# First stage of a decoder layer: weights and x in halves, other loads later, zero products and one SiLU ahead

## The reference

```
v = silu(dwconv_causal(x @ v_w.T, convv_w))      # 4 taps per channel, 256 channels
short = dwconv_causal(v, fir_s)                   # 3 taps
# long_ and wide: 31 and 64 taps of the same v; then delta rule on q, k, v, gate, mixing
x = layernorm(x + attn(x)); x = layernorm(x + xattn(x, ctx)); x = layernorm(x + ffn(x))
```

## Time and profile before

| what | value |
|---|---|
| median of three runs | 664.91 us (664.7 to 665.05) |
| profiled execution: span from first to last instruction | 663.7 us |
| the profiled execution's own time | not given apart; the median is 1.2 us above its span |
| first matmul / first ACT work / first DVE work | 7.64 / 11.45 / 13.58 us |
| PE starts the second stage | 61.47 us |

### The profile page before, as it was taken

How to read it: one execution, slowest core, us unless ns; L and a number is a source line. 1 busy time by engine, 2 the same in 40 slices (tenths; PEclk the granted TensorE clock), 3 DMA queues, 4 the chain that set the end, 5 groups by cost and what they waited for, 6 DMA issues and landing times.

```text
span 663.7 us, 16965 instructions
## 1 busy us (share of the span) xinstructions
PE 570.7 (86%) x7446; PEld 409.4 (62%) x7446; DVE 464.9 (70%) x898; ACT 281.7 (42%) x510; POOL 118.1 (18%) x102
## 2 busy tenths in 40 slices
PE   4886889898998999887998867799999799879983
PEld 1454567676767667765544445688888665446542
DVE  1986857867786787854859999364266875676674
ACT  1766545433452344332365542333322545444541
POOL 1001520250061016000011223353000000000000
PEclk9898979999999999987999888799999899989998
DMA  6600710330051014120421117100000000000001
GB/s 182 222 3 2 232 55 4 122 105 4 8 178 44 4 34 129 35 99 34 172 84 32 33 32 243 32 1 0 1 1 1 1 0 1 1 32 1 33 21 44
DMA packets 26536, 37.50 MB, mean 57 GB/s; under 512 B 4641, under 2 KB 13602, under 8 KB 26463
## 3 DMA queue, kind: packets, MB, share of 16 engines
q1 hardware_dynamic: 26463, 36.42, 17.1%
HBM read 34.31 MB, written 2.10 MB: 55 GB/s over the span
## 4 chain that ended last, share of the span: by engine, by line
PE 20%; DVE 17%; ACT 6%; issue 6%; POOL 1%; POOLq 0%; DVEq 0%
PE bank L1805 6%; PE bank L1787 3%; PE bank L1862 2%; DVE arena L2502 2%; DVE arena L2509 2%; PE bank L1876 2%; ACT arena L2192 2%; ACT arena L2194 1%; DVE arena L2279 1%; PE bank L1908 1%; DVE arena L149 1%; ACT short L2098 1%; DVE arena L2318 1%; PE bank L1808 1%; PE bank L690 1%
## 5 line engine op out<-in xcount | busy, mean ns | idle before, releaser
L298 DVE SCALAR_TENSOR_TENSOR arena<-bank,conv_w,arena 128x511 f32<-128x511 f32 (+2 forms) x72 | 53.1, 746 | 17.3 <-ACT arena L457 14.0
L1523 POOL COPY arena<-v_win 128x256 f32<-128x256 f32 x32 | 20.2, 660 | 171.7 <-PE bank L775 171.7
L2055 ACT COPY arena<-bank 128x512 f32<-128x512 f32 x40 | 23.3, 584 | 56.0 <-PE bank L1805 37.1
L1805 PE MATMUL bank<-v_win,arena 128*128 128x256 f32 x192 | 46.0, 389 | 0.0
L1920 PE MATMUL bank<-v_win,arena 128*128 128x256 bf16 x288 | 36.1, 277 | 8.3 <-DVE arena L2522 7.3
L1190 ACT COPY arena<-bank 128x512 f32<-128x512 f32 x40 | 21.7, 589 | 48.2 <-PE bank L901 48.2
L1805 PEld LDWEIGHTS bank<-v_win,arena 128*128 128x128 f32 x192 | 37.3, 196 | 5.6 <-issue 0.4
L1787 PE MATMUL bank<-v_win,arena 128*128 128x256 f32 x128 | 33.5, 425 | 7.7 <-DVE arena L2348 4.4
L775 PE MATMUL bank<-arena 128*32 128x128 f32 x512 | 35.7, 409 | 4.9 <-ACT arena L1140 3.1
L1908 PE MATMUL bank<-arena,v_win 128*128 128x512 bf16 x144 | 35.9, 386 | 3.8 <-DVE arena L2502 1.7
L1920 PEld LDWEIGHTS bank<-v_win,arena 128*128 128x128 bf16 x288 | 28.1, 99 | 17.1 <-DVE arena L2522 8.2
(11 more groups left out here) (284 smaller groups left out, 1345.0 us busy)
## 6 DMA issues: line engine op xcount, KB each, us to landing
arena<-in_toep_w SPq DMA_DIRECT2D x32, 256.0 KB, 3.0
arena<-in_toep_l SPq DMA_DIRECT2D x32, 256.0 KB, 3.9
arena<-in_xT SPq DMA_DIRECT2D x12, 512.0 KB, 4.7
arena<-in_x SPq DMA_DIRECT2D x4, 512.0 KB, 4.0
arena<-in_ctx SPq DMA_DIRECT2D x4, 512.0 KB, 4.2
out<-arena SPq DMA_DIRECT2D x4, 512.0 KB, 2.9
qkv_w<-in_qkv_wT SPq DMA_DIRECT2D x1, 768.0 KB, 5.4
v_win<-in_w_gateT SPq DMA_DIRECT2D x1, 768.0 KB, 4.7
```

What stands on the lines that cost most here:

```text
L298: return nc.vector.scalar_tensor_tensor(out=acc[:, j:L], in0=src[:, 0:L - j], scalar=conv_w[:, m, CONV_K - 1 - j:CONV_K - j], in1=acc[:, j:L],
L1805: i = mm(oo, src[:, k, f * P:(f + 1) * P], w[:, k, :], start=(k == 0), stop=(k == KT - 1 and f > 0))
L2055: nc.scalar.copy(dst(i), bank[RING_FIRST + n % RING].rearrange("p (t c) -> p t c", c=dst(i).shape[-1]))\
```

## The change

The changed kernel issues the first loads in another order and in smaller pieces, each with its own semaphore:

- The value columns of the weights and x of batch 0 are fetched in halves by channel group k (128 KB and 256 KB), and PE's first projection waits for each half just before the matmul that reads it.
- `conv_w` stands between the halves; `short_w` and the identity come after x of batch 1. ACT and DVE wait for `conv_w` and `short_w`; PE waits for the identity only at `turn_v(0)`.
- The key and query columns of the weights are fetched after x of batch 2, and both before the small weights; PE waits for them at `project_keys(0)`.
- DVE first writes zeros to a tile `unused`; PE then multiplies it by itself eight times into a bank that is not in use yet; ACT applies one SiLU to one column of it.

```
-                load_xT(0)
-                sp.dma_start(qkv_w[:], dr["qkv_wT"].rearrange("(k p) n -> p k n", p=P)).then_inc(first_loaded.sem, 16)
-                sp.dma_start(conv_w[:], dr["conv_w"].rearrange("(m p) j -> p m j", p=P)).then_inc(first_loaded.sem, 16)
-                sp.dma_start(short_w[:], dr["fir_s"].rearrange("(k p) j -> p k j", p=P)).then_inc(first_loaded.sem, 16)
-                sp.dma_start(ident[:], dr["c_ident"]).then_inc(first_loaded.sem, 16)
+                for k in range(KT):
+                    rows = slice(k * P, (k + 1) * P)
+                    sp.dma_start(qkv_w[:, k, 2 * D:3 * D], dr["qkv_wT"][rows, 2 * D:3 * D]).then_inc(s1[f"first_in{k}"].sem, 16)
+                    sp.dma_start(A1[0]["xT"][:, k, :], dr["xT"][0][rows, :]).then_inc(s1[f"first_in{k}"].sem, 16)
+                    if k == 0:
+                        sp.dma_start(conv_w[:], dr["conv_w"].rearrange("(m p) j -> p m j", p=P)).then_inc(s1["taps_in"].sem, 16)
                 load_xT(1)
+                sp.dma_start(short_w[:], dr["fir_s"].rearrange("(k p) j -> p k j", p=P)).then_inc(s1["taps_in"].sem, 16)
+                sp.dma_start(ident[:], dr["c_ident"]).then_inc(s1["ident_in"].sem, 16)
                 for n in const:
                     if n != "ident":
                         load(const[n][:], dr["c_" + n])
+                sp.wait_ge(s1["proj"].sem, s1["proj"].at(0, 2))
+                load_xT(2)
+                sp.dma_start(qkv_w[:, :, 0:2 * D], dr["qkv_wT"][:, 0:2 * D].rearrange("(k p) n -> p k n", p=P)).then_inc(s1["keys_in"].sem, 16)
...
-                for b in range(2, B):
-                    sp.wait_ge(s1["proj"].sem, s1["proj"].at(b - 2, 2))
-                    load_xT(b)
+                sp.wait_ge(s1["proj"].sem, s1["proj"].at(1, 2))
+                load_xT(3)
...
                     for k in range(KT):
+                        if n == 0:
+                            pe.wait_ge(s1[f"first_in{k}"].sem, 32)
...
+                    if b == 0:
+                        pe.wait_ge(s1["ident_in"].sem, 16)
...
+                        pe.wait_ge(s1["keys_in"].sem, 16)
...
-                pe.wait_ge(first_loaded.sem, 16 * 4)
+                def idle_products():
+
+                    pe.wait_ge(s1["primed"].sem, 1)
+                    for _ in range(IDLE_PRODUCTS):
+                        nc.tensor.matmul(bank[7][:, 0:P], unused[:, :, :].rearrange("p a c -> p (a c)"),
+                                         unused[:, :, :].rearrange("p a c -> p (a c)"), start=True, stop=True)
+
+                idle_products()
...
-                act.wait_ge(first_loaded.sem, 16 * 4)
+                act.wait_ge(s1["primed"].sem, 1)
+                a(scratch, unused[:, 0, 0:1], ACT.Silu).then_inc(s1["primed"].sem, 1)
+                act.wait_ge(s1["taps_in"].sem, 32)
...
-                dve.wait_ge(first_loaded.sem, 16 * 4)
+                v.memset(unused[:, :, :].rearrange("p a c -> p (a c)"), 0.0).then_inc(s1["primed"].sem, 1)
+                dve.wait_ge(s1["taps_in"].sem, 32)
```

More of the change, by code:

```diff
@@ L42 @@
 TOEP_BUFS = 4
+IDLE_PRODUCTS = 8
 HALF = L // 2
@@ L238, in layer @@
         half_exp = sb("half_exp", [P, 2, 16])
-        first_loaded = Signal(ctx.enter_context(nc.semaphore("first_loaded")), 0)
         dc_loaded = Signal(ctx.enter_context(nc.semaphore("dc_loaded")), 0)
@@ L293, in layer @@
             "v_out": 4, "sh_out": 2, "sh_conv": 6, "v_squared": 2, "sh_squared": 2, "sums": 1, "rows_out": 1, "rows_turned": 1,
-            "sums_out": 1, "pads": 0}, ())
+            "sums_out": 1, "pads": 0, "first_in0": 0, "first_in1": 0, "taps_in": 0, "ident_in": 0, "keys_in": 0, "primed": 0}, ())
         def tap_one(nc, acc, src, m, j):
@@ L353, in project @@
                     b, m = n // KT, n % KT
-                    if m == 0:
-                        pe.wait_ge(s1[f"xT_in{b % 2}"].sem, s1[f"xT_in{b % 2}"].at(b // 2, 16))
+                    if m == 0 and b:
+                        pe.wait_ge(s1[f"xT_in{b % 2}"].sem, 32 if b == 3 else 16)
                     if n >= 3:
```

## The result

| | before | changed |
|---|---|---|
| median | 664.98 us | 655.12 us (651.53 to 656.14, 4 runs) |
| profiled execution: its time, its span | not given, 663.7 | 654.44, 652.3 |
| ratio to before | | 0.9844 [0.98, 0.9888] |

Some 10 us are there each time.

The account below looks back on a forecast made before the run. DVE was taken to set the first stage, the only one edited: 5.4 us from its earlier start plus 2.2 from stalls, so 663.7 - 7.6 + 1.2 = 657.3 us; own range 656.5 to 658.2, whole range 655.6 to 660.4.

Parts of the forecast that it names:

- the clock raised by zeros: First stage, start: eight zero products let PE's second-half records run at full speed, 1.2 us, ending at 7.0.
- the stalls 0.95 and 0.40 gone and 1.64 kept: DVE's waits in the first stage: earlier x of batch 2 removes the first two; the last, at PE-ACT ping-pong, stays.
- First data and the gate: First stage, start: second half landed at 5.8, short_w gating ACT and DVE at 7.15; DVE starts 5.4 us earlier.
- The 1.01 goes, bar 0.14: DVE's third stall, waiting for the SiLUs of batch 2 in the first stage: 0.87 us saved, 0.14 kept.
- Whatever comes earlier there moves the rest of the program along unchanged: Barrier before PE's second stage: the stage's 7.6 us carry to the end, unless a later transfer or the clock objects.
- the clock elsewhere: Rival, later stages: one PE spell of 3.4 us at low clock comes or goes, up to 1.7 us; chance 0.08.
- I take those 1.2 us as what lies around the span: Whole kernel: median 664.91 less the span 663.7, taken as time outside the span and left unchanged.
- About 0.2%, 1.3 us, is what a measurement of this kernel can tell: Whole kernel: smallest difference told from no change, with three runs within 0.35 us.
- The high end of the whole range, 660.4: Whole kernel: slowest time in the range, said to take a slow start together with the stalls.
- stalls that stay: Rival, first stage: x of batch 2 or the SiLUs come late; gain 5.4 alone, 659.5; chance 0.13.
- slow products: Rival, first projection: zeros don't raise PE's clock, DVE starts at 8.8, 658.0; chance 0.15.
- late short_w: Rival, ACT and DVE's gate: short_w follows its issue, or 1 KB rows are slow; DVE at 9.6, 658.7; chance 0.15.

Follow-up runs that it names:

- late_x2: Changed kernel with the loads of x of batch 2 and the key weights put back behind the small loads: 662.79 us, ratio 0.997.
- x2_only: Kernel before with one edit, the load of x of batch 2 moved in front of the small loads: 663.26 us, ratio 0.999.
- best: Changed kernel with short_w right behind conv_w, x of batch 3 right behind the key weights, sixteen zero products after PE's last key projection: 654.49 us.
- primed_only: Kernel before with only the zeros, the eight zero products and the one SiLU at the start, loads as before: 665.49 us, ratio 1.0029.
- after_fourth: Changed kernel, unedited, timed and profiled again: 654.65 us, ratio 0.9846.

## Why the prediction was wrong in size

**Right.** The order of events came as forecast: the table load hidden; the clock raised by zeros; x of batch 2 issued at 9.47 (9.4) and there at 13.90 (13.5 to 15.3); the stalls 0.95 and 0.40 gone and 1.64 kept; nothing waited for the key weights or the small loads. late_x2 and x2_only show that the stalls went because of that load.

**First data and the gate: mis-sized.** Forecast were a second half landed at 5.8, short_w at 7.15, and DVE at 8.1 to 8.2. They came at about 6.6, 8.1 and 8.99: the start gained 4.6, not 5.4. The windows' 390 and 418 GB/s belong to rows of 2 and 3 KB; while the halves of the weights with their 1 KB rows, conv_w's pieces and the x halves passed, 200 and 232 were measured. The trace's packets name one part: 731 of conv_w's 768 pieces pass between 3 and 4 us, at 9 ns each, which over the 16 DMA engines is 0.41 us of that one; 0.27 had been put for it. What the 1 KB rows cost apart from that, no run separates. And short_w was neither bound by bytes alone (7.15) nor by its issue (8.65): it landed 4.5 us after its issue at 3.65, in between.

**"The 1.01 goes, bar 0.14": mis-sized.** 0.71 stayed. I followed the SiLUs of batch 2 from batch 2's own chain and didn't ask for the transfer after that: x of batch 3 is still behind twelve small loads, and projection 6 waited for it until 23.91. best, with that load earlier, has no such stall, though its stage ended no earlier for it (54.96).

The stage thus gave 6.4 in the first profile (4.8 to 6.6 over five) where 7.6 stood.

**"Whatever comes earlier there moves the rest of the program along unchanged": this step failed.** Behind the stage another 5.0 us came by the first pair of profiles, 4.6 by the medians of five comparisons. I had the mechanism among the rivals (*the clock elsewhere*), but as one spell coming or going, up to 1.7 us, with 0.08. It is several spells. That it is the clock in the main: take off what a clock below 1 costs behind the stage, by the trace's clock record, from the part of the span behind the stage. The kernel before has 602.2 - 27.6 = 574.6, the changed kernel's five profiles 575.3, 573.2, 577.7, 576.7 and 577.3, none of them shorter beyond 1.4 us. So there is no less work behind the stage, only less of it at 1.2 GHz. Over all executions it looks alike: the mean times less the mean cost of the clock are 638.0 us before and 632.1 changed, 5.9 apart, as much as the stage gave. This takes the whole cost as lost time. It isn't all of it, since PE isn't the bound everywhere: between executions of one kernel, a us of this cost goes with 0.5 to 0.6 us of time. By that measure the 4.0 us less of it stand for 2.1 to 2.4 us. And about 1 us of the 4.0 lies within the first stage, by the profiles. So the clock accounts for some 1.6 to 3 us of the 4 behind the stage in these means; the rest isn't shown.

What makes it is settled in part. Shown: PE idle ahead of stage two costs clock behind it. A delay of 6.4 us there costs 9.9 on an idle PE and 5.9 with PE kept busy, and keeping PE busy there in the kernel before wins 3.1 behind an unchanged stage. Shown too: in the changed kernel the gain behind the stage hangs on the eight zero products, worth 6.5 us. Why primed_only has none of it is known as far as its first step: there the products didn't raise the clock of projection 0. Open: how products that end at 4.6 make stretches at 1.2 GHz rarer hundreds of us later. Nor do the gains add up: sixteen products at the boundary win 3.1 before and nothing in the changed kernel. The changed kernel without its products has 1.6 to 2.8 more behind the stage than the kernel before, and late_x2, whose stage ends late, has the gain: so an earlier end of the stage alone isn't what brings it, as far as a column good to some 2 us can tell.

**"I take those 1.2 us as what lies around the span": wrong, and harmless.** For one and the same execution time less span is 2.1. The kernel before's profiled execution thus took 665.8, 0.9 above its median, and the 1.2 took that off again. It explains why the spans differ by 11.4 and the medians by 9.9: 0.9 there, and the changed kernel's profiled execution 0.7 below its median.

**"About 0.2%, 1.3 us, is what a measurement of this kernel can tell": wrong.** It was read off three executions that happened to lie within 0.35 us. The 107 later ones of the kernel before lie up to 12.3 us apart, and the 95% intervals of the ratios are 0.4 to 1.1% wide. The forecast's own range of 1.7 us was narrower than the spread of the changed kernel's five medians, 2.7 us. The high end of the whole range, 660.4, doesn't follow from its terms either: stalls that stay give 660.2 with slow products and 660.9 with a late short_w.

## What to carry to other kernels

An earlier start is worth what the next late transfer lets it be: here the place of one load, and the key weights behind it, decided over 6.5 of some 10 us, so follow each later load to its reader before summing. A forecast that shifts the rest of a PE-bound program "unchanged" needs a clock term of several us in 660, in both directions; read the granted clock in windows far behind the edit, over several profiles, and try short zero products where PE idles, with and without them on one chip. See that they reach the first real product: in primed_only they ended 2.6 us ahead of it and changed nothing. One profile of such a kernel isn't enough: its executions lie 4 to 12 us apart, and in the main the time goes with the mean clock.

## What was not expected of the hardware

- Eight products of zeros at 1.05 to 4.6 us changed the median by 6.5 us, with the first stage of the same length (55.37 and 55.47), and the mean cost of the clock from 25.8 to 22.6 us; the same products in the kernel before, followed by 2.6 us of idle time, left even the next product at half speed.
- The granted-clock column reads 1.00 in the windows from 3 to 5 us, while the first products run at half rate. The clock record of a trace begins only where the clock first rises (4.2 us into the span in the changed kernel's first profile, 11.2 in the kernel before's, where the spacing of the weight loads halves), and the column counts what lies ahead of it as 1.00. There the spacing (0.85 against 0.43) has to be read.
- Halves of 128 and 256 KB together with 12 KB in small pieces passed at 200 to 232 GB/s, where whole 512 and 768 KB transfers passed at 390 to 418. A piece of 16 bytes held a DMA engine for 9 ns, a row of 2 KB for 84 to 102 ns (changed kernel, from 3 us on).
- A projection that starts after 4.5 or 9 us of waiting takes 3.7 to 3.8 us instead of 1.98. So did one of 3.57 us behind a wait of only 1.47 in after_fourth, where the other profiles have 1.98 behind waits of 1.14 to 1.32.
